# Products of ones in TensorE's first waits, and the 512-column sums of W0 moved ahead of the small sums

## The reference, cut to what matters

```
h   = gelu(cond @ W0 + b0);  h = gelu(h @ W1 + b1)
att = softmax(h @ W2 + b2)                       # 128 x 8
c0  = einsum('boi,bih->boh', att*weight, x) + (att @ bias_k)[:, :, None]
x   = x + c0 @ W_base.T + b_base + 4 active experts of rank 8, softmax over them
c1  = grouped conv(x, 9 taps, 4 groups) + (c @ c_weight.T)[:, :, None] + bias
x   = x + c1 @ base_W.T + top-2 of 28 experts of rank 8
```

## Time and profile before

| | us |
|---|---|
| median of 3 runs | 400.69 |
| the 3 runs | 396.14, 400.69, 404.12 |
| the profiled execution's own time | 401.4 |
| its span | 399.4 |
| TensorE busy | 382.2 (96% of the span) |
| VectorE busy | 285.8 (72%) |
| ScalarE busy | 120.8 (30%) |
| GpSimd busy | 31.3 (8%) |
| mean granted TensorE clock | 0.97 |

### The profile page before, as it was taken

How to read it: one execution, slowest core, us unless ns; L and a number is a source line. 1 busy time by engine, 2 the same in 40 slices (tenths; PEclk the granted TensorE clock), 3 DMA queues, 4 the chain that set the end, 5 groups by cost and what they waited for, 6 DMA issues and landing times.

```text
span 399.4 us, 9569 instructions
## 1 busy us (share of the span) xinstructions
PE 382.2 (96%) x3187; PEld 334.6 (84%) x3187; DVE 285.8 (72%) x973; ACT 120.8 (30%) x378; POOL 31.3 (8%) x111
## 2 busy tenths in 40 slices
PE   5999799999999999999999999999999999999876
PEld 4889777888888898888888889888888889977764
DVE  4557849777777787777677787777777778777754
ACT  5334523323322333222332233322332223222310
POOL 5246000000000000000000000000000000000000
PEclk8559989999999999999999999999999999999999
DMA  7843807566667677666566767766666676766651
GB/s 217 264 146 88 203 28 181 122 168 165 157 163 184 162 180 184 150 154 162 156 163 163 184 158 184 177 155 149 157 167 160 167 184 132 160 159 155 139 107 53
DMA packets 70716, 62.97 MB, mean 158 GB/s; under 512 B 3823, under 2 KB 53199, under 8 KB 70570
## 3 DMA queue, kind: packets, MB, share of 16 engines
q1 hardware_dynamic: 70696, 62.74, 64.4%
q10 hardware_dynamic: 2, 0.00, 0.0%
HBM read 45.69 MB, written 16.91 MB: 157 GB/s over the span
## 4 chain that ended last, share of the span: by engine, by line
PE 84%; DVE 7%; DMA 5%; issue 1%; ACT 1%; SPq 1%; DVEq 0%; ACTq 0%
PE p_chy L883 13%; PE p_chy L877 13%; PE p_chy L878 13%; PE p_u L877 9%; PE p_u L883 9%; PE p_u L878 8%; PE p_chy L1013 7%; PE p_t L1026 3%; DMA win<-x_scratch 3%; PE p_y L877 2%; PE p_y L878 2%; PE p_y L883 2%; DMA w_sb<-in_w 1%; DMA x_scratch<-x 1%; PE p_chy L946 1%
## 5 line engine op out<-in xcount | busy, mean ns | idle before, releaser
L877 PE MATMUL p_u<-w_hi,xt_hi 128*128 128x256 f32 (+1 forms) x256 | 70.7, 302 | 3.6 <-DVE w_lo L638 3.6
L878 PE MATMUL p_u<-w_lo,xt_hi 128*128 128x256 f32 (+1 forms) x256 | 68.3, 293 | 0.0
L744 DVE STREAM_TRANSPOSE c<-p_chy 128x512 f32<-128x512 f32 x32 | 22.9, 717 | 55.3 <-PE p_chy L1013 54.9
L504 ACT CAST u_hi<-p_u 128x256 fp32r<-128x256 f32 x64 | 24.7, 386 | 104.4 <-PE p_u L883 104.3
L877 PEld LDWEIGHTS p_u<-w_hi,xt_hi 128*128 128x128 f32 x256 | 49.4, 193 | 4.5 <-issue 2.8
L546 ACT CAST g1t_hi<-p_t 113x256 fp32r<-113x256 f32 x32 | 11.9, 373 | 125.2 <-PE p_t L1026 125.2
L878 PEld LDWEIGHTS p_u<-w_lo,xt_hi 128*128 128x128 f32 x256 | 49.6, 194 | 0.0
L877 PE MATMUL p_chy<-w_hi,c_hi 128*128 128x512 f32 x124 | 49.3, 397 | 0.0
L878 PE MATMUL p_chy<-w_lo,c_hi 128*128 128x512 f32 x124 | 48.8, 394 | 0.0
L883 PE MATMUL p_u<-w_hi,xt_lo 128*128 128x256 f32 (+1 forms) x256 | 43.9, 294 | 0.4 <-DVE xt_lo L619 0.4
L1013 PEld LDWEIGHTS p_chy<-win,wc_sb 96*32 96x32 f32 x1024 | 26.0, 109 | 14.5 <-issue 10.1
(11 more groups left out here) (169 smaller groups left out, 758.1 us busy)
## 6 DMA issues: line engine op xcount, KB each, us to landing
win<-x_scratch SPq DMA_DIRECT2D x96, 256.0 KB, 4.4
x_scratch<-x SPq DMA_DIRECT2D x32, 260.0 KB, 2.1
xt_sb<-in_xt SPq DMA_DIRECT2D x32, 256.0 KB, 5.2
x_sb<-in_x SPq DMA_DIRECT2D x32, 256.0 KB, 5.2
out<-y_sb SPq DMA_DIRECT2D x32, 256.0 KB, 4.5
w_sb<-in_w SPq DMA_DIRECT2D x4, 256.0 KB, 5.3
w_sb<-in_w SPq DMA_DIRECT2D x1, 1024.0 KB, 6.4
a_sb<-in_a SPq DMA_DIRECT2D x1, 504.0 KB, 4.0
```

What stands on the lines that cost most here:

```text
L504: nc.scalar.copy(u_hi[:, t.mod(4), cols], p_u[:, banks]).then_inc(u_hi_done[half], 1)
L744: V.transpose(c1[:], p_cv).then_inc(c1_tr, 1)
L877: mm(psum, lhs_hi, rhs_hi, start=start and n == 0, stop=False)
L878: mm(psum, lhs_hi, rhs_lo, start=False, stop=False)
```

## The change

A helper `keep_busy(n)` issues n products of ones (128 x 128 weights, 128 columns, from `ones_r`) into the columns 0 to 127 of `p_u`, which no other work uses then and nobody reads. It is called with 2 behind the products for `beta1`, with 3 behind the net's second layer, with 8 behind its third, and with 6 behind the first chunk of tile 0. The wait for `ones_r_done` moves to the front. The 512-column sums move from behind `vrow` to directly behind half "a" of tile 0, ahead of `beta0`, the small sums and `vrow`; their wait for `beta1_done` moves with them. No instruction of another engine changes.

```diff
@@ -910,6 +910,13 @@
             for _ in range(5):
                 mm(p_u[:, 0:P], ones[:], ones[:], start=True, stop=True)
 
+            def keep_busy(n):
+
+                for _ in range(n):
+                    mm(p_u[:, 0:P], ones_r[:], ones_r[:], start=True, stop=True)
+
+            pe.wait_ge(ones_r_done, 1)
+
             pe.wait_ge(ld_pack, 16)
             cond = pack_sb[:, C_COND:C_COND + BATCH]
             mm(p_mlp, pack_sb[:, C_W0:C_W0 + P], cond, start=True, stop=True).then_inc(u1_mm, 1)
@@ -919,10 +926,13 @@
                 last = mm(p_beta1[by_batch[b]], pack_sb[:, C_CW:C_CW + CH],
                           cond.rearrange("p (t b) -> p b t", b=BT)[:, b, :], start=True, stop=True)
             last.then_inc(beta1_mm, 1)
+            keep_busy(2)
             pe.wait_ge(m1_done, 1)
             mm(p_mlp, pack_sb[:, C_W1:C_W1 + P], m1[:], start=True, stop=True).then_inc(u2_mm, 1)
+            keep_busy(3)
             pe.wait_ge(m2_done, 1)
             mm(p_am, m2[:], pack_sb[:, C_W2:C_W2 + MK], start=True, stop=True).then_inc(am_mm, 1)
+            keep_busy(8)
 
             first = Tile(None, 0)
             banks, cols = HALVES["b"]
@@ -935,6 +945,7 @@
 
             after(pe, xt_hi_done, first)
             first_chunk(0)
+            keep_busy(6)
             first_chunk(1)
             pe.wait_ge(ident_done, 1)
             pe.wait_ge(att_done, 1)
@@ -951,16 +962,15 @@
             lo_passes(p_u[:, banks], u_operands(first, cols), True).then_inc(u_mm["b"], 1)
             pe.wait_ge(a0_lo_done, 1)
             u_half(first, "a")
+            pe.wait_ge(beta1_done, 1)
+            column_sums(p_rsw0, P, w0_hi[:, :, Z0N:Z0N + D], w0_lo[:, :, Z0N:Z0N + D]).then_inc(rsw0_mm, 1)
             for b in range(BT):
                 last = mm(p_beta0[by_batch[b]], kw_sb[:, CH * CH:CH * CH + CH],
                           att_t[:].rearrange("k (t b) -> k b t", b=BT)[:, b, :], start=True, stop=True)
             last.then_inc(beta0_mm, 1)
-            pe.wait_ge(ones_r_done, 1)
             column_sums(p_rs0, P, w0_hi[:, :, 0:Z0N], w0_lo[:, :, 0:Z0N]).then_inc(zrow_mm, 1)
             pe.wait_ge(vact_done, ACT0)
             mm(p_vrow, ones[0:1, :], vact[:], start=True, stop=True).then_inc(vrow_mm, 1)
-            pe.wait_ge(beta1_done, 1)
-            column_sums(p_rsw0, P, w0_hi[:, :, Z0N:Z0N + D], w0_lo[:, :, Z0N:Z0N + D]).then_inc(rsw0_mm, 1)
```

## The result

| | before | changed |
|---|---|---|
| median of 12 runs, us | 399.49 | 402.99 |
| lowest and highest, us | 396.14, 404.12 | 399.41, 405.19 |
| profiled execution's own time, us | 401.4 | 400.96 |
| its span, us | 399.4 | 398.9 |

The ratio is 1.0104, with a 95% interval of 1.0067 to 1.0141: the change makes the kernel 1% slower, 3.5 us by the medians. A second comparison gave 1.0091 (1.0039 to 1.0142). Of 93 runs of the kernel before that stood beside the experiments, 33 took under 399 us; of the 24 runs of the changed kernel none did.

A forecast was written before the change was run, and what follows sets the result against it. TensorE, busy 96% of the span, and its clock were taken to bound the kernel. 401.4 + 0.1 (products of ones) - 0.5 (G) + 1.7 (clock fall) = 402.7; the median lies 0.7 below, so 402.0 us, range 396.3 to 406.

The forecast's parts named there:

- The products of ones: TensorE's early waits: nineteen products, nearly all covered by waiting, cost 0.1 us and do not hold the clock up.
- the first rival: Products of ones hold the clock from 4.4 us, or it is up by 12; 396 to 397.6 us; chance 0.18.
- G: Time at which step 0's transpose (line 990) can start on TensorE: 30.0 us instead of 30.47, a gain of 0.5.
- The rise of the clock: TensorE's clock returns to full at about 21 us, after wide products in a row from 15.77, instead of about 28.3.
- that case, with +1.5 us: Runs whose clock rose at 19 already: `vrow` comes at 23.2 instead of 21.6; the change costs 1.5 us.
- The stall and the fall: TensorE waits 3.5 us for `g0s` before step 0's transpose instead of 0.84; the clock then falls, costing 1.7 us.
- The long fall: Rival: clock falls in the new stall and stays low through the busy stretch from 30.0; 409.2 us; chance 0.06.
- the clock that holds: Rival: the clock stays up through the new stall before step 0's transpose; 400.3 us; chance 0.2.
- the rival in which the rise stays at 28.3: Sums move but no clock is won; `vrow` at 26.2, G at 32.3; 402.6 to 403.6 us; chance 0.08.
- my first suspect: Rise and falls of TensorE's clock, suspected as what separates runs of the kernel before, 396.14 to 404.12 us.

The follow-up runs named there:

- two of its variants: Against the kernel before: the moved sums without products of ones, 1.0075; the changed kernel with eight fp32 products of ones for its nineteen, 1.0018.
- the pair: Second traces of the unaltered changed kernel and kernel before, clock rising at 19.2 and 19.7 us; ratios to the kernel before 1.0091 and 0.9969.

## Why the prediction was right, and where its sum was off

The time, 402.99 us, lies in the range and 1 us above the forecast of 402.0. The forecast was for a small loss that can't be told from nothing at 2%, and so it came. That the number is so near is in part luck. The sum made the change cost 1.3 us, and by the medians it costs 3.5. Of the 2.2 us between them 1.2 were made good by the base: the median of the three runs it stood on, 400.69, is that much above the median of the twelve. What held is the mechanism: `vrow` behind the moved sums, VectorE's queue in front of z0, the long stall, the fall of the clock, in this order.

- **The products of ones**: as predicted. They did not hold the clock: it falls between 7.7 and 8.5 us in three traces with them, in the other three their pitch is that of the half clock from 4.5 us on, and line 957 takes 3.75 to 3.78 us in all six. Line 957 starts at 11.45 to 11.81 us in these, within what line 946 did without them (11.40 to 12.06), so they are covered as predicted; their ratio is 1.0033, with nothing and 0.7% both in the interval. The prediction leaned on the small sums as their nearest kin and on line 946, and did not know what would hold the clock. The fp32 products show that the clock can be held until line 957, so the first rival failed through the kind of product. It can't be the waits that were left: the changed kernel with fp32 products waited 0.23, 0.63 and 0.92 us before 10 us, no less than the changed kernel itself (0.17 and 0.66), and its clock fell at 11.7 instead of 7.7. That rival's G, 25.7, is near the 25.0 measured with them in the old order. The Trainium skill, "TensorE: Matmul & The Clock Gate", Part 1, says that activity releases the throttle; with the fp32 products the traces agree (0.99 over 4 to 13 us in one of them), with the nineteen short ones they don't.
- **The rise of the clock**: put at 21 us, found at 18.0 and 19.2. Both are before the moved sums begin, and in the kernel before it came at 19.7 in its second trace. In these three executions the move was not needed for it. Over all traces it may have been of use: of the five in the old order without fp32 products two have the rise only at 27.9 and 28.3, and none of the seven with the sums moved has it later than 20.7. These are too few to be sure.
- **G**: this is the term that was mis-sized. The sum took -0.5 us, against an execution in which the clock had stayed low to 28.3. Against that same execution it measures 28.56 - 30.47 = -1.9, since the rise came 3 us earlier than put. Against one in which it rose at 19.7 the term is +1.6. The prediction had named that case, with +1.5 us, but made its sum without it. G before is 30.47 in one trace and 27.47 in the other, so the profiled execution was no fair base. Set beside it, the changed kernel's own profiled execution was not slower at all (401.4 and 400.96).
- **The stall and the fall**: predicted 3.5 us of wait, measured 3.32 to 3.35 in four traces, both of the changed kernel and two of its variants. The fall was put at 1.7 us; between G and step 1's transpose it costs 2.80 - 1.59 = 1.2 us in the pair. With G's 1.6 that is 2.8 us of the measured 3.5. The rest is not settled. It is within the interval (2.7 to 5.6 us, from 0.67% and 1.41% of 399.49). The prediction took it from the stall of 2.49 us in its trace that a fall had followed; that was not sure to come, since of the eleven traces in which this later stall stands unfilled six have no fall there.
- **The long fall** and **the clock that holds** did not appear in any trace of the changed kernel: in both of them the clock fell in or just behind the stall and was low for 3.4 us.
- **Two slips of the sum**: for the rival in which the rise stays at 28.3 the time with a fall is 401.4 + 0.1 + 1.8 + 1.7 = 405.0, not 404.3, and the best end of the first rival against the median is 395.9, not 396.3. Neither bears on the result.

What separates executions of one kernel was "my first suspect" in the prediction; the traces bear it out in part. In the pair of second traces the whole stretch from step 1 to tile 31 takes the same time, and what differs in and between the traces is the clock up to 33 us, at step 2's stall near 50, and behind 377. How much of the spread of the 93 runs that makes was not worked out.

## What to carry to other kernels

When work is moved on one engine to sit better for that engine, look for what stands behind the last result that another engine waits for: here 3 us of VectorE's queue had been running beside the moved work, and the move put them one behind the other. Work whose result nobody needs soon (the 512-column sums) is the cover for a round trip, so it belongs behind the product that starts the round trip. Before a sum is made against one profiled execution, look whether the clock in it rose or fell by chance. Where it did, make the sum a second time for the other case.

## What the runs showed of the hardware that was not expected

- Nineteen products of 128 columns in the rounded 4-byte type left the clock to fall at 7.7, 8.1 and 8.5 us in the three traces in which it was up at all; without them it fell at 7.8, 8.0 and 8.0. With eight fp32 products of the same shape in the same places it fell at 11.7, 11.7 and 12.8 us. What in the fp32 product makes the difference was not tested.
- Line 957, 8 rows deep, kept TensorE busy without a gap, and the clock fell during it (at 11.7, 11.7 and 12.8 us in the three traces with the fp32 products) or did not rise.
- Stalls of 1.93 and 1.98 us left the clock up in two traces and one of 1.99 us was followed by a fall in another; the same stall of 2.48 to 2.49 us at step 2 was met or followed by a fall in five traces and left the clock up in six; 3.3 us were followed by a fall, in or just behind them, in every one of the four traces with such a stall.
